# A two-block kernel of dense and low-rank layers: the opening's loads, its tables of places, and the last output tile in two halves

## What is computed

```python
xn = _layernorm(x, axis=-1)
x = x + _L0_attn_ref(xn, ...) + _L0_ffn_ref(xn, ...)
xn = _layernorm(x, axis=-1)
x = x + _L1_attn_ref(xn, ...) + _L1_ffn_ref(xn, ...)
```

## Time and profile before

| | |
|---|---|
| median of 3 runs | 274.3 us (273.87 to 275.35) |
| the profiled execution's own time | 274.41 us |
| its span, first to last instruction | 271.6 us |
| PE busy | 262.9 us, 97% of the span |
| POOL / DVE / ACT busy | 148.4 / 188.1 / 129.3 us |
| transferred | 17.86 MB in 12037 packets |

### The profile page before, as it was taken

How to read it: one execution, slowest core, us unless ns; L and a number is a source line. 1 busy time by engine, 2 the same in 40 slices (tenths; PEclk the granted TensorE clock), 3 DMA queues, 4 the chain that set the end, 5 groups by cost and what they waited for, 6 DMA issues and landing times.

```text
span 271.6 us, 4677 instructions
## 1 busy us (share of the span) xinstructions
PE 262.9 (97%) x1678; PEld 136.9 (50%) x1678; DVE 188.1 (69%) x299; ACT 129.3 (48%) x222; POOL 148.4 (55%) x182
## 2 busy tenths in 40 slices
PE   7599999999999999999999999999999999999994
PEld 2395455555545555555454554564444445444441
DVE  4688878968865888686888678888568595533314
ACT  2524487736455246574767451450176412356500
POOL 5987945396731172628456563414189990066920
PEclk9999999999999999999999999999999999999999
DMA  6999997101020010300120203100200002200004
GB/s 196 275 287 244 255 207 125 40 2 31 7 80 1 2 39 0 80 0 0 40 80 17 68 1 118 39 0 2 61 18 0 0 4 77 80 0 0 0 0 154
DMA packets 12037, 17.86 MB, mean 66 GB/s; under 512 B 880, under 2 KB 6768, under 8 KB 12016
## 3 DMA queue, kind: packets, MB, share of 16 engines
q1 hardware_dynamic: 6624, 12.23, 14.0%
q0 software_dynamic: 4960, 4.98, 11.5%
q10 hardware_dynamic: 432, 0.38, 0.4%
HBM read 20.46 MB, written 2.10 MB: 83 GB/s over the span
## 4 chain that ended last, share of the span: by engine, by line
PE 92%; DMA 3%; DVE 1%; ACT 1%; SPq 1%; issue 0%; DVEq 0%
PE bank L745 18%; PE bank L629 18%; PE bank L628 18%; PE bank L596 9%; PE bank L598 9%; PE bank L597 9%; DMA stage<-in_gate 3%; PE bank L676 3%; PE bank L590 2%; PE bank L707 2%; PE bank L697 1%; PE bank L696 1%; PE bank L665 1%; DVE X L1181 1%; PE bank L684 1%; PE bank L718 1%
## 5 line engine op out<-in xcount | busy, mean ns | idle before, releaser
L1302 POOL TENSOR_TENSOR hidl<-hid,hidh 128x512 f16<-128x512 f32 x28 | 33.0, 1178 | 31.3 <-ACT hidh L811 31.1
L628 PE MATMUL bank<-xh,gatew 128*128 128x512 f16 (+1 forms) x136 | 43.8, 341 | 2.2 <-ACT gatew L852 2.2
L628 PE MATMUL bank<-xh,upw 128*128 128x512 f16 (+1 forms) x136 | 43.9, 341 | 0.0
L629 PE MATMUL bank<-xl,upw 128*128 128x512 f16 (+1 forms) x136 | 43.8, 341 | 0.0
L629 PE MATMUL bank<-xl,gatew 128*128 128x512 f16 (+1 forms) x136 | 43.8, 341 | 0.0
L745 PE MATMUL bank<-downw,hidh 128*128 128x512 f16 x112 | 42.5, 379 | 0.0
L745 PE MATMUL bank<-downw,hidl 128*128 128x512 f16 x112 | 42.4, 379 | 0.0
L1206 POOL TENSOR_TENSOR root<-var,powers 128x4 f32<-128x4 f32 (+1 forms) x25 | 23.8, 956 | 31.8 <-DVE var L1048 31.2
L1308 POOL TENSOR_TENSOR actl<-hid,acth 128x512 f16<-128x512 f32 (+1 forms) x22 | 25.5, 1165 | 25.8 <-ACT acth L818 25.4
L906 ACT ACTIVATE silu<-bank,early 128x512 f32<-128x512 f32 x28 | 19.3, 688 | 27.4 <-PE bank L629 26.6
L1169 DVE SCALAR_TENSOR_TENSOR hid<-bank,early,silu 128x512 f32<-128x512 f32 (+1 forms) x22 | 16.5, 750 | 18.3 <-ACT silu L921 15.6
(11 more groups left out here) (183 smaller groups left out, 563.0 us busy)
## 6 DMA issues: line engine op xcount, KB each, us to landing
X<-in_x SPq DMA_DIRECT2D x7, 256.0 KB, 11.9
downw<-in_down POOLq DMA_DIRECT2D x2, 896.0 KB, 19.0
out_x<-X SPq DMA_DIRECT2D x7, 256.0 KB, 2.0
stage<-in_v SPq DMA_DIRECT2D x6, 256.0 KB, 2.7
gatew<-in_gate POOLq DMA_DIRECT2D x1, 1024.0 KB, 15.0
upw<-in_up POOLq DMA_DIRECT2D x1, 1024.0 KB, 19.5
stage<-in_mask SPq DMA_DIRECT2D x4, 256.0 KB, 2.7
stage<-in_weight SPq DMA_DIRECT2D x4, 256.0 KB, 3.0
```

Source lines behind the costliest of these rows:

```text
L628: pe.matmul(bank_of(key)[:, c], w, xh[b][:, k, c], start=(k == 0), stop=False)
L629: mm = pe.matmul(bank_of(key)[:, c], w, xl[b][:, k, c], start=False, stop=(k == KT - 1))
L1302: pool.tensor_tensor(hidl[:, n % FT, :], hid[:, n % UNITS, :], hidh[:, n % FT, :], ALU.subtract).then_inc(hid_lo, 1)
```

## The change

The change does five things.

1. POOL's first two code loads are no longer issued ahead of its roots: `load 1` (up) comes behind the third root, `load 0` (gate) behind `grow 1`.
2. Six code tiles are staged by SP and cast by ACT in place of four (`gate` and `up` 2 are new), in a ring of seven slots in place of five; POOL's first loads carry tiles 3 to 6 in place of 2 to 5.
3. PE's opening has 18 matmuls on constants ahead of its first transposes in place of 15 and 5 between; the steps `first` stand in another order.
4. Of the last half's outputs, three are finished ahead of the last tile, and the last tile is worked in two halves of 256 columns, the second in a bank of its own. DVE adds each half by itself, and SP and ACT each wait for their half alone.
5. Every table of places is new; with it the stats of the second half and their roots come ahead of `rows` and `winparts`, and the first rotation table (`table 0`) comes ahead of the scans with more steps between.

```diff
-FIRST_LOADS = 4
-NSTAGE = 5
+FIRST_LOADS = 6
+NSTAGE = 7
...
-    dense += [("attn", 1, 1), ("hidden_end", 1), ("attn", 1, 2), ("zcopy", 1), ("attn", 1, 3)]
-    dense += [("out", 1, t) for t in range(TPB)]
+    dense += [("attn", 1, 1), ("hidden_end", 1), ("zcopy", 1), ("attn", 1, 2)]
+    dense += [("out", 1, t) for t in range(TPB - 1)] + [("attn", 1, TPB - 1), ("out", 1, TPB - 1)]
...
-CODE_LOADS = (("gate", 2, 6), ("up", 2, 6), ("gate", 6, 14), ("up", 6, 14), ("down", 0, 7), ("down", 7, 14))
+CODE_LOADS = (("gate", 3, 7), ("up", 3, 7), ("gate", 7, 14), ("up", 7, 14), ("down", 0, 7), ("down", 7, 14))
...
-LN_AT = (1.9, 2.8, 3.3, 4.2, 6.4, 10.4, 10.8, 12.3, 13)
-TABLE_AT = (7.6, 14.9, 24.8, 52.7)
+LN_AT = (0, 0, 0, 0, 0, 0, 3.2, 5.2, 9.1)
+TABLE_AT = (5.5, 15.3, 19.6, 52.9)
...
+            if step == ("attn", NBLK - 1, TPB - 1):
+                take(("tail",))
...
+        def halves(key):
+
+            if key == ("attn", NBLK - 1, TPB - 1):
+                return [(key, slice(0, D // 2)), (("tail",), slice(D // 2, D))]
+            return [(key, slice(0, D))]
...
-            for t in range(NTOK // P):
+            for t in range(NTOK // P - 1):
                 sp.wait_ge(out_ready, t + 1)
-                c = slice(0, D // 2) if t == NTOK // P - 1 else slice(0, D)
-                sp.dma_start(out[t][:, c], X[:, t, c]).then_inc(out_done, 16)
+                sp.dma_start(out[t], X[:, t, :]).then_inc(out_done, 16)
+            sp.wait_ge(last_ready, 1)
+            sp.dma_start(out[NTOK // P - 1][:, 0:D // 2], X[:, NTOK // P - 1, 0:D // 2]).then_inc(out_done, 16)
...
-                    for k in range(KT):
-                        three_passes(bank_of(step)[:], [yh[b][:, k, c], yl[b][:, k, c]],
-                                     [Wh[:, k, :], Wl[:, k, :]], k == 0, False)
+                    if b * TPB + t == NTOK // P - 1:
+                        wait_bank(pe, ("tail",))
+                    for key, n in halves(step):
+                        for k in range(KT):
+                            three_passes(bank_of(key)[:, n], [yh[b][:, k, c], yl[b][:, k, c]],
+                                         [Wh[:, k, n], Wl[:, k, n]], k == 0, False)
...
-            act.wait_ge(out_ready, last + 1)
+            act.wait_ge(last_ready, 2)
...
-                    wait_full(dve, ("attn", b, t))
-                    emit(dve.tensor_tensor(X[:, n, :], X[:, n, :], bank_of(("attn", b, t))[:],
-                                           ALU.add), out_ready)
+                    for key, c in halves(("attn", b, t)):
+                        wait_full(dve, key)
+                        emit(dve.tensor_tensor(X[:, n, c], X[:, n, c], bank_of(key)[:, c], ALU.add),
+                             last_ready if n == NTOK // P - 1 else out_ready)
```

More of the change, by code:

```diff
@@ L172, in build_order @@
     return order
[L175 to L180, removed]
+PROLOGUE = (("seed", 0), ("fill", 3), ("codes", "up", 1), ("stats", 0), ("codes", "gate", 1), ("xt", 0), ("root", 0),
+            ("stats", 1), ("root", 1), ("xt", 1), ("stats", 2), ("norm", 0), ("seed", 1), ("root", 2), ("first", 0,
+            1), ("first", 0, 0), ("norm", 1), ("stats", 3), ("xl", 0), ("load", 1), ("root", 3), ("codes", "gate", 0),
+            ("norm", 2), ("offset", 3), ("seed", 2), ("xl", 1), ("codes", "up", 0), ("xl", 2), ("norm", 3), ("xt", 2),
+            ("xt", 3), ("first", 1, 0), ("first", 1, 1), ("grow", 0), ("first", 2, 1), ("codes", "up", 2), ("grow",
+            1), ("codes", "gate", 2), ("load", 0), ("first", 2, 0), ("grow", 2), ("grow", 3), ("first", 3, 0), ("xl",
+            3), ("first", 3, 1))
 ACT_NORMS = (3,)
@@ L203 @@
-WOUT_AT = (23.9,)
[L204 to L214, removed]
+LOAD_AT = (0.4, 1.8, 1.8, 10.8)
+GROW_AT = (0, 0, 0, 0.4, 0.4, 0.8)
+LN_AT = (0, 0, 0, 0, 0, 0, 3.2, 5.2, 9.1)
+TABLE_AT = (5.5, 15.3, 19.6, 52.9)
+XT_AT = (7, 7.8, 9.1, 10.4)
@@ new lines @@
+PREP_AT = (1, 2.7, 3, 3.6)
+W1_AT = (10.5, 45.6)
+W2_AT = (14.3,)
+WOUT_AT = (23.9,)
+XBIAS_AT = (24.8, 72.8)
+MASK_AT = (24.1, 45.9, 52, 56.4, 62)
+U1_CAST_AT = (17.1,)
+V1_AT = (55.3, 57.2, 77, 80.1, 83.1, 85)
+U2_AT = (86.5, 91.7, 94.4)
+CHAIN_AT = ((8.1, 9.3, 11.8, 12.8, 13.1, 13.5, 14.2, 14.9, 17.5, 18.1, 19.9, 19.9, 22, 23.7, 25.9, 25.9, 26.3, 28.5, 29.4, 29.8, 31, 31.9, 33.7, 34.4, 37.1, 37.9, 40.7, 41.1, 41.7, 41.7, 44.6, 45.8, 47.1, 47.9, 49.5, 50.4, 52.4, 52.7, 55.4, 55.9, 56.7, 57.2, 60.5, 61.9, 63.3, 63.4, 65, 66.1, 68.2, 69.7, 71, 72.5, 73.7, 75), (14, 16, 19.8, 19.8, 21.2, 22.6, 24.3, 25.6, 27.2, 29.1, 30, 30.7, 32.4, 34.1, 34.3, 34.7, 35, 35.6, 38.7, 39.7, 41.2, 41.4, 43.3, 44.3, 46.1, 47.3, 48.3, 48.6, 50.1, 50.4, 52.4, 54, 55.8, 56.8, 59.2, 59.7, 62.7, 63, 64.1, 64.2, 65.7, 66.3, 68.4, 69.8, 71.7, 72.5, 74, 74.8, 76, 78.2, 80.6, 82.3, 84.7, 84.7))
@@ L217, in place_psum @@
+WMASK_AT = (64.5, 65.7, 82.8, 86.1)
+W_AT = (84.1, 85.8, 86.6, 93.3)
+LN1_AT = ((74.1, 74.6, 76.1, 76.8, 76.8, 79.1, 79.1, 79.7, 79.7, 81, 81.5, 81.5, 81.5), (89.3, 94, 101.2, 101.5, 102.5, 102.5, 102.7, 104.5, 104.5, 104.5, 104.5, 104.7, 105))
+YBIAS_AT = ((109.1, 109.1, 109.1, 109.2), (123.7, 123.7, 127.8, 129.9))
+V2_AT = (102.4,)
 def place_psum(order):
@@ L431, in two_layers @@
         out_ready, out_done, last_done, x0_in = sem("out_ready"), sem("out_done"), sem("last_done"), sem("x0_in")
+        last_ready = sem("last_ready")
         down_read = sem("down_read")
@@ L798, in _ @@
                     c = slice(t * P, (t + 1) * P)
-                    key = ("attn", b, t)
-                    three_passes(bank_of(key)[:], [zh[:, c], zl[:, c]], split["V2"],
-                                 False, True).then_inc(full_of(key), 1)
+                    for key, n in halves(("attn", b, t)):
+                        three_passes(bank_of(key)[:, n], [zh[:, c], zl[:, c]], [w[:, n] for w in split["V2"]],
+                                     False, True).then_inc(full_of(key), 1)
         @block.scalar
```

6 lines of the change are left out of this document (removed).

## The result

| | before | with the change |
|---|---|---|
| median | 274.52 us (273.54 to 275.41, 7 runs) | 272.88 us (272.22 to 273.62, 7 runs) |
| profiled execution: own time, span | 274.41, 271.6 us | 272.88, 270.8 us |
| time outside the span | 2.8 us | 2.1 us |

The ratio is 0.9949, with a 95% interval from 0.9928 to 0.9970: faster by half a per cent, at the edge of what a measurement of this kernel can tell, and the interval reaches to both sides of that edge. The prediction was 272.4 us.

A forecast was written before the change was run, and what follows sets the result against it. PE bounds the kernel: its start, a fixed number of matmul columns, and what follows the last matmul. -2.0 - 0.4 + 0.2 + 0.3 = -1.9 gave 272.4 us against 274.3, range 271.4 to 274.5.

The forecast's parts named there:

- gate 1's landing: In the opening, SP's transfers up to gate 1 take 4.7 us from about 2.5: landing near 7.5, against 11.2 before.
- The front, -2.0: In the opening, `first` begins at 10.0 and gate 2 starts at 18.4 instead of 20.41: 2.0 us won.
- The end, -0.4: Behind the last matmul, three adds are already done, so the last store is issued at 268.7: 0.4 us won.
- Codes at gate 3, +0.2: At gate 3, wanted at 21.9, loads end at 20.8 to 21.8: a wait of 0 to 0.5 us, taken as 0.2.
- The rival by which the second load takes 11.0 us again: At gate 3, POOL's second load lands at 25.7, PE waits 3.8 us, time 276.0; chance 0.08.
- `t1`, +0.3: At the first `t1`, its root stands behind three `hidl` on POOL: ready at 35.8, wanted at 35.5, 0.3 us of wait.
- `table 0` clear of POOL's subtractions: At the first rotation table, the new place matters 0.2 us at most on DVE, beside PE's work.
- It fits with 0.2 to spare: At gate 4, the third silu ends at 26.0 and its bank is wanted at 26.2, so no wait.
- no wait is added: In the rest of the chain, shortest distances are 3.0 to 6.7 us; unnamed small waits go into the range, 0 to 1.5.
- no other wait over 0.3: Sign to look for: apart from waits near 21.9 and 35.5, PE has none over 0.3 us up to the end.
- new waits in the dense stretch, of 0.5 to 1.5 us: Rival: waits by banks or POOL's turn in PE's dense stretch, 0.5 to 1.5 us in all, time 273.0 to 274.0; chance 0.18.

The follow-up runs named there:

- Experiment 3: The changed kernel with the old end: last tile in one piece, four outputs in a row; 273.34 us, ratio to before 0.9970.
- Experiment 4: The changed kernel with four code tiles staged instead of six, POOL's first loads carrying tiles 2 to 5 at their new places; 277.11 us, ratio to before 1.0081.
- experiment 1: The changed kernel with the first rotation table moved from 5.5 to 9.25, behind the fourth and fifth `hid`; 271.78 us, ratio to before 0.9905.
- experiment 9: The changed kernel with the first table at 9.25, `attn(1,0)` ahead of the second block's `hidden`, POOL's third load at 8.2; 270.52 us, ratio to before 0.9856.

## Why the prediction was right, and where it was not

The time is inside the range and 0.5 us above the forecast; the span, 270.8, is 1.1 above the forecast 269.7. The sum behind it was right at both ends and wrong in the middle. Two sums on the way are slightly off and change nothing: 2.5 + 4.7 puts gate 1's landing at 7.2 and not 7.5, and the root for `t1` adds up to 35.7 and not 35.8.

- **The front, -2.0.** Measured -1.93, and by the mechanism given: `first` at 10.05 (predicted 10.0) behind `xl`, gate 2 at 18.48 (18.4).
- **The end, -0.4.** From the last matmul to the store 0.98 us instead of 1.46; less the 0.11 by which the last matmul starts later, that is 0.37 up to the issue. The store then lands 0.27 sooner, which the sum did not have. Experiment 3 puts the whole at 0.5 to 0.6 us. Right, if a little low.
- **Codes at gate 3, +0.2.** No wait in this profile, 0.6 in that of experiment 3. The landing at 21.7 lies in the predicted 20.8 to 21.8. The rival by which the second load takes 11.0 us again did not occur: issued near 14.5, it took 6.7 to 8.0 us in every trace. Experiment 4 shows that its danger was real, at gate 2 instead of 3.
- **`t1`, +0.3.** Measured 0.32 (the starts 36.82 and 37.36 lie 0.54 apart instead of 0.22). But experiment 1 shows that the term was too small: without the hold-up at gate 5, which delays the demand as well, `t1` waits 0.6 to 0.8.
- **The step that failed** is "`table 0` clear of POOL's subtractions: 0.2 us at most on DVE, beside PE's work". The place that the prediction did work out, at gate 4 ("It fits with 0.2 to spare"), held: gate 4 starts at 26.26 without a wait. One tile on, at gate 5, it put the cost at nothing ("no wait is added") and expected "no other wait over 0.3". I took the change's own words for what it does. The order has the table ahead of the scans, but in time it lies on `hidl`, and its three operations take 4.57 us in place of 1.41. The fourth `hid` stands behind them on DVE, gate 5 behind that: 1.45 us, by the distance of starts 31.56 (the last of four that begin at 31.23, 0.11 apart) and 33.12, less the usual 0.11. I had counted columns between jobs at their usual durations, which can't see that. It is the mechanism and the size of the rival "new waits in the dense stretch, of 0.5 to 1.5 us", which had a chance of 0.18; the time stayed under its 273.0 to 274.0.
- **The forecast was near only by luck.** The parts give -1.93 + 1.45 + 0.32 - 0.37 - 0.27 = -0.80, the fall of the profiled span from 271.6 to 270.8. The time fell by 1.6. The other 0.8 was in no term of the sum, and it hid more than half of the 1.45 that was missed. Part of it lies in which execution of before was profiled. Over the executions of the experiments' four comparisons, before's median span is 272.0 to 272.3, not 271.6. The time outside the span was 2.8 us in the profiled execution; it is over 2.3 us in 19 of before's 62 executions and 1.8 to 2.2 in the others. In the changed kernel and the ten variants that keep the new end it is over 2.3 in 1 of 75. With the old end back, in experiment 3, it is 2.5 to 2.8 in 3 of 12. So the longer time outside the span seems to go with the old end; its mechanism isn't traced, and nor is the longer span.

The rows for the failed step were in the trace of before. These are DVE's normalisations of the second block, and POOL's operations beside them:

```profile
217.66 4.24 DVE L989 TENSOR_SCALAR XN<-X,mv,root 128x512 f32<-128x512 f32 x3 [1.18 <-POOL root L1206]
```

```profile
217.53 1.26 POOL L1296 TENSOR_TENSOR bias<-bias 128x512 f32<-128x512 f32 x1
218.87 2.75 POOL L1298 TENSOR_TENSOR X<-X,bias 128x512 f32<-128x512 f32 x2
```

Three operations that took 0.55 us each in the opening took 1.4 each here. A group's mean hides it; the same line at two places shows it.

## What to carry to other kernels

Before you place a DVE operation that reads SBUF, look at what POOL runs at that moment. Price it as these traces show: one of 0.42 us ends 0.3 us behind the end of POOL's operation (one of 0.69 us, `W1l`, 0.56 us behind in experiment 9), and behind the last of several without a gap. A gain ahead of a stretch with no slack counts only as far as the first queue behind it is still on time: compare the length of that stretch, between two named instructions, in both traces. And when a change pays for one wait with another, try its parts one number at a time: here one number gave 1.1 us, and two numbers and one step moved gave 2.4.
